# Soft mixture-of-experts logits: factor applied to phi's columns in place of the products, softmaxes on the products in PSUM, division by the sums moved to the combine stage

## The chip, the core and the metric

One Trainium2 chip; the program runs on one core. The metric is the device time of one execution in microseconds (us). The time given for a kernel is the median of its runs; one further execution is recorded by the hardware profiler.

## What is computed

The program takes 1250 nodes of 768 features (`x`) and a list of 40000 edges and puts four layers one after another, each added to x: a graph attention layer, a soft mixture of experts, a graph convolution and a top-2 mixture of experts. The change is inside the second, which is, cut to what matters:

```python
# x: 1250 x 768 rows after layer norm; phi: 768 x 32 experts x 32 slots; EPS = 1e-12
xn = l2norm(x, axis=2)
phin = scale * l2norm(phi, axis=0)
logits = einsum('bld,des->bles', xn, phin)
d_w = softmax(logits, axis=-1)                        # over the 32 slots of an expert
c_w = softmax(logits.reshape(b, l, E * S), axis=-1)   # over all 1024
slots = einsum('bld,bles->besd', xn, d_w)
h = gelu(einsum('besd,edh->besh', slots, w1) + b1, approximate=False)
eo = (einsum('besh,ehd->besd', h, w2) + b2).reshape(b, E * S, d)
out = einsum('bkd,blk->bld', eo, c_w)
```

## The kernel before

The kernel is written engine by engine: in each stage a function opens a scope of buffers and semaphores and gives every engine its own list of instructions, with the waits between engines written by hand. At the end of a scope the semaphores are cleared and all engines meet in a barrier (`Scope.clear`, L93). Nothing is scheduled by a planner; the order on each engine is the order of the text, and a wait holds up everything behind it on its engine. TensorE is PE, VectorE is DVE, ScalarE is ACT in what follows.

The rows are tiled as 10 blocks (`NB`) of 128 nodes, the features as 6 slices (`KD`) of 128, and the 1024 slots (`SE`) are the columns. The soft mixture consists of these stages:

- `norm_rows` (L357) makes layer norm and l2 norm of the rows in `R.H`.
- `soft_logits` (L1045) loads phi in 6 slices into `ph` (the tile `slotsT`, later overwritten with the slots) and makes both softmaxes. Its result is `disp`, 10 blocks of 128x1024, and `comb`, the same shape.
- `soft_slots` (L1192) multiplies `R.H` and `disp` to the slots and at its start has the first hidden weights loaded.
- `soft_experts` (L1222) runs the 32 experts in 8 groups of 4, with their weights loaded group by group, the outer ones into the room of `disp`. Its output `eo` is in `R.H`.
- `soft_combine` (L1328) turns each block of `comb` and multiplies it with `eo`; DVE adds the products to `R.X` (L1359).

In `soft_logits` the sum of squares of each column of phi comes first: ACT squares each slice (L1120), PE adds over the partitions with a matrix of ones into the bank pair `psO[1]` (L1151). DVE clips it (L1076), ACT takes the root (L1137), and DVE makes the factor r of each column: a reciprocal (L1081), a correction step (L1082 to L1085) and the scale (L1087). r is the same on all partitions.

The loop over blocks has two slots, s = 0 and 1, each with its own rows, turned rows and PSUM banks. The order on each engine for a block b is:

- PE: transposes of the next block's rows (`turn`, L1157), then 12 matmuls of 128x512 (24 records in the profile) of turned rows and phi into `psO[s]` (`multiply`, L1165). Before them it waits for the turned rows (`s_turned`) and for `s_scaled` >= b + 1, which DVE raises with L1095 of block b - 2, that is when it has taken over the products of the block that used this bank pair. The first two counts come from a bare increment at the start and from the clip.
- ACT: the copy of rows two blocks ahead (L1124), the copy of the turned rows (L1127), then the two exponentials of block b: of all 1024 logits less the row's maximum into `comb`, with their sum in `rs` (L1131), and of the logits less each expert's maximum, in `disp` (L1132). It waits for DVE's subtraction (`s_sub`).
- DVE: the products times r into `sq` (L1095), each expert's maximum (L1099), the row's maximum (L1100) and its negation (L1101), the subtraction (L1102); a wait for both exponentials (`s_exp`); the sum over each expert (L1105), its reciprocal (L1106), the division of `disp` (L1107); the reciprocal of the row's sum (L1108) and the division of `comb` (L1109). `Chain` puts a semaphore wait behind an instruction whose result the next one on the same engine needs; `chain.loop(i, n)` counts these per turn of the loop.

Of the kernel before, what the change touches and what calls it, by code (L numbers as in the profile page):

```python
# [16 lines left out]
ALU = mybir.AluOpType  # L17
# [1024 lines left out]
HC = HID // 2  # L1042


def soft_logits(nc, R, name, phi, scale, disp, comb, ph):  # L1045

    with Scope(nc, name) as c:
# [2 lines left out]
        ones, sc = c.sb("ones", [P, P]), c.sb("scale", [P, 1])  # L1052
        rows = [c.sb(f"rows{s}", [P, D]) for s in range(2)]
        rowsT = [c.sb(f"rowsT{s}", [P, KD, P]) for s in range(2)]
        gm, rm, gs, rs = c.sb("gm", [P, 2, EXPERTS, 1]), c.sb("rm", [P, 2]), c.sb("gs", [P, 2, EXPERTS, 1]), c.sb("rs", [P, 2])
        psT = [c.ps(f"psT{s}", [P, 2, BANK]) for s in range(2)]
        psO = [c.ps(f"psO{s}", [P, 2, BANK]) for s in range(2)]
        s_w = [c.sem(f"weights{k}") for k in range(KD)]
        s_sc, s_v, s_sq, s_n, s_clip, s_root = (c.sem(x) for x in ("scale", "v", "sq", "n", "clip", "root"))
        s_rows, s_turn, s_turned, s_mm, s_scaled, s_exp, s_sub = (c.sem(x) for x in ("rows", "turn", "turned", "mm", "scaled", "exp", "sub"))  # L1060
        block = c.enter_context(nc.Block())

        @block.sync
# [5 lines left out]
        @block.vector  # L1069
        def _(dve):  # L1070
            chain = Chain(dve, s_v)
            chain(nc.vector.memset(ones[:], 1.0))
            dve.sem_inc(s_scaled, 1)
            dve.wait_ge(s_n, KD)
            n2, r = f[:, 0, :], f[:, 1, :]
            chain(nc.vector.tensor_scalar(n2.rearrange("p (a b) -> p a b", a=2), psO[1][:], 1e-24, None, ALU.max))  # L1076
            dve.sem_inc(s_scaled, 1)
            dve.sem_inc(s_clip, 1)
            dve.wait_ge(s_root, 1)

            chain(nc.vector.reciprocal(r, sq[:, 0, :]))  # L1081
            chain(nc.vector.tensor_tensor(sq[:, 1, :], r, r, ALU.mult))  # L1082
            chain(nc.vector.tensor_tensor(sq[:, 1, :], sq[:, 1, :], n2, ALU.mult))
            chain(nc.vector.tensor_scalar(sq[:, 1, :], sq[:, 1, :], -0.5, 1.5, ALU.mult, ALU.add))
            chain(nc.vector.tensor_tensor(r, r, sq[:, 1, :], ALU.mult))  # L1085
            dve.wait_ge(s_sc, 16)
            chain(nc.vector.tensor_scalar(r, r, sc[:], None, ALU.mult))  # L1087

            with dve.Fori(0, NB // 2) as i:
                chain.loop(i, 14)  # L1090
                for s in range(2):

                    b = i * 2 + s
                    dve.wait_ge(s_mm, b + 3)
                    nc.vector.tensor_tensor(sq[:, s, :].rearrange("p (a e) -> p a e", a=2), psO[s][:], r.rearrange("p (a e) -> p a e", a=2), ALU.mult).then_inc(s_scaled, 1)  # L1095
                    dve.wait_ge(s_scaled, b + 3)
                    lg = sq[:, s, :].rearrange("p (e s) -> p e s", e=EXPERTS)
                    dsp = blk(disp, b).rearrange("p (e s) -> p e s", e=EXPERTS)
                    chain(nc.vector.tensor_reduce(gm[:, s], lg, AX.X, ALU.max))  # L1099
                    chain(nc.vector.tensor_reduce(rm[:, s:s + 1], gm[:, s].squeeze(2), AX.X, ALU.max))  # L1100
                    chain(nc.vector.tensor_scalar(rm[:, s:s + 1], rm[:, s:s + 1], -1.0, None, ALU.mult))  # L1101
                    nc.vector.tensor_tensor(dsp, lg, gm[:, s].broadcast_to([P, EXPERTS, SLOTS]), ALU.subtract).then_inc(s_sub, 1)  # L1102
                    dve.wait_ge(s_exp, b * 2 + 2)
                    dve.nop(nofuse=True)
                    chain(nc.vector.tensor_reduce(gs[:, s], dsp, AX.X, ALU.add))  # L1105
                    chain(nc.vector.reciprocal(gs[:, s], gs[:, s]))  # L1106
                    nc.vector.tensor_tensor(dsp, dsp, gs[:, s].broadcast_to([P, EXPERTS, SLOTS]), ALU.mult)  # L1107
                    chain(nc.vector.reciprocal(rs[:, s:s + 1], rs[:, s:s + 1]))  # L1108
                    chain(nc.vector.tensor_scalar(blk(comb, b), blk(comb, b), rs[:, s:s + 1], None, ALU.mult))  # L1109
            chain.end(NB // 2)  # L1110

        @block.scalar
        def _(act):
            act.sem_inc(s_turn, 2)
            act.sem_inc(s_mm, 2)
            for k in range(KD):
                act.wait_ge(s_w[k], 16)
                if k >= 2:
                    act.wait_ge(s_n, k - 1)
                nc.scalar.activation(sq[:, k % 2, :], ph[:, k, :], ACT.Square).then_inc(s_sq, 1)  # L1120

            def turn(b, s):
                act.wait_ge(s_turn, b + 1)
                nc.scalar.copy(rows[s][:], blk(R.H, b)).then_inc(s_rows, 1)  # L1124
                act.wait_ge(s_turn, b + 3)
                act.wait_ge(s_mm, b + 1)
                nc.scalar.copy(rowsT[s][:].rearrange("p (a k) q -> p a (k q)", a=2), psT[s][:, :, 0:HALF]).then_inc(s_turned, 1)  # L1127

            def exponentials(b, s):
                act.wait_ge(s_sub, b + 1)  # L1130
                nc.scalar.activation(blk(comb, b), sq[:, s, :], ACT.Exp, bias=rm[:, s:s + 1], accum_out=rs[:, s:s + 1]).then_inc(s_exp, 1)  # L1131
                nc.scalar.activation(blk(disp, b), blk(disp, b), ACT.Exp).then_inc(s_exp, 1)  # L1132

            turn(0, 0)
            turn(1, 1)
            act.wait_ge(s_clip, 1)
            nc.scalar.activation(sq[:, 0, :], f[:, 0, :], ACT.Sqrt).then_inc(s_root, 1)  # L1137
            with act.Fori(0, NB // 2 - 1) as i:
                for s in range(2):
                    turn(i * 2 + s + 2, s)  # L1140
                    exponentials(i * 2 + s, s)
            for s in range(2):
                exponentials(NB - 2 + s, s)

        @block.tensor
        def _(pe):
            pe.wait_ge(s_v, 1)
            for k in range(KD):
                pe.wait_ge(s_sq, k + 1)
                for a in range(2):  # L1150
                    last = nc.tensor.matmul(psO[1][:, a, :], ones[:], sq[:, k % 2, a * BANK:(a + 1) * BANK], start=(k == 0), stop=(k == KD - 1))  # L1151
                last.then_inc(s_n, 1)

            def turn(b, s):
                pe.wait_ge(s_rows, b + 1)
                for k in range(KD):
                    last = nc.tensor.transpose(psT[s][:, k // 3, (k % 3) * P:(k % 3 + 1) * P], rows[s][:, k * P:(k + 1) * P], R.ident[:])  # L1157
                last.then_inc(s_turn, 1)

            def multiply(b, s):  # L1160
                pe.wait_ge(s_turned, b + 1)
                pe.wait_ge(s_scaled, b + 1)
                for a in range(2):
                    for k in range(KD):
                        last = nc.tensor.matmul(psO[s][:, a, :], rowsT[s][:, k, :], ph[:, k, a * BANK:(a + 1) * BANK], start=(k == 0), stop=(k == KD - 1))  # L1165
                last.then_inc(s_mm, 1)

            turn(0, 0)
            with pe.Fori(0, NB // 2 - 1) as i:
                turn(i * 2 + 1, 1)  # L1170
                multiply(i * 2, 0)
                turn(i * 2 + 2, 0)
                multiply(i * 2 + 1, 1)
            turn(NB - 1, 1)
            multiply(NB - 2, 0)
            multiply(NB - 1, 1)

# [147 lines left out]
                last.then_inc(s_e, 1)  # L1325


def soft_combine(nc, R, name, comb, eo):  # L1328

    with Scope(nc, name) as c:  # L1330
        rows = [c.sb(f"rows{s}", [P, SE]) for s in range(2)]
# [19 lines left out]
        @block.vector  # L1351
        def _(dve):
            dve.sem_inc(s_add, 2)
            with dve.Fori(0, NB // 2) as i:
                for s in range(2):
                    b = i * 2 + s
                    dve.wait_ge(s_mm, b + 3)
                    x = blk(R.X, b).rearrange("p (a d) -> p a d", a=2)
                    nc.vector.tensor_tensor(x, x, psO[s][:, :, 0:HALF], ALU.add).then_inc(s_add, 1)  # L1359

        @block.tensor
        def _(pe):
# [4 lines left out]
                last.then_inc(s_turn, 1)  # L1367

            def multiply(b, s):
                pe.wait_ge(s_add, b + 1)  # L1370
                pe.wait_ge(s_turned, b + 1)
                for a in range(2):
                    for k in range(KS):
# [760 lines left out]
def program(nc, A, out):  # L2134
    with ExitStack() as ctx:
# [51 lines left out]
        norm_rows(nc, R, "ln1", l2=True)  # L2187
        with ExitStack() as soft:
            comb = soft.enter_context(nc.sbuf_tensor("comb", [P, NB, SE], F32))
            slotsT = soft.enter_context(nc.sbuf_tensor("slotsT", [P, KD, SE], F32))  # L2190
            disp = soft.enter_context(nc.sbuf_tensor("disp", [P, NB, SE], F32))
            soft_logits(nc, R, "m1", A["L0_ffn_phi"], A["L0_ffn_scale"], disp, comb, slotsT)
            eo = R.H
            with Scope(nc, "hw") as c:
                hidden_weights = HiddenWeights(c, A["L0_ffn_w1"])
                soft_slots(nc, R, "m2", disp, slotsT, hidden_weights)
                soft_experts(nc, R, "m3", hidden_weights, A["L0_ffn_b1"], A["L0_ffn_w2"], A["L0_ffn_b2"], slotsT, eo, disp[:])
            soft_combine(nc, R, "m4", comb, eo)
        with ExitStack() as gcn:
            R.high = gcn.enter_context(nc.sbuf_tensor("high", [P, NB, D], FR))  # L2200
            R.low = nc.alloc_sbuf_tensor_at("low", [P, NB, D], FR, offset=h_at)
# [39 lines left out]
```

## Time and profile before

| what | value |
|---|---|
| median of 3 runs | 4810.34 us (4807.37 to 4814.28) |
| the profiled execution, time | 4806.03 us |
| its span, first to last instruction | 4803.5 us |
| mean granted clock of PE | 0.922 of full speed |
| PE busy, share of the span | 3900.7 us, 81% |
| DVE busy | 2679.1 us, 56% |
| ACT busy | 1793.9 us, 37% |
| POOL busy | 1492.7 us, 31% |

The page gives shares over the whole span; the stages have very different limits, so it is the stage that is to be read. In the rows below, a line of a timeline reads: start in us from the span's start, duration in us, engine, line of the kernel, operation, output<-inputs, count, and in brackets the engine's idle time before it with what ended that. A line of the windows reads: stretch, its length, then busy us (and count) of PE, PE's weight loads, DVE, ACT and POOL, the granted clock of PE as a share of full speed, the share of DMA and GB/s. A line of the groups reads: line, engine, operation, output<-inputs with shapes, count, busy us, mean ns of one, idle time before them with its releasers. Ends of PE's matmuls are modelled.

### The profile page before, as it was taken

The page shows a single profiled execution, that of the slowest core. Times are in us where ns is not written, and L with a number is a line of the kernel's source. Part 1 is how long each engine was busy: PE and PEld are TensorE (multiplying, and loading weights), DVE is VectorE, ACT ScalarE, POOL GpSimd, SP SyncE. Part 2 cuts the span into 40 slices and gives each one's busy share as a digit, 9 for nine tenths or more (in the row PEclk, how much of TensorE's full clock was granted, in tenths as well). Part 3 has the DMA queues.
Part 4 walks back from the last instruction along what each step waited for, and adds up shares of the span by engine and source line. Part 5 has one row for each costly group of instructions (what it writes and reads, how often), then busy time and mean ns, then how long its engine had stood idle before and what let it go on. Part 6 is the DMA issues. An engine that isn't in the chain of part 4 may idle for free. (4 is left out here: it accounts for less than half of the span.)

```text
span 4803.5 us, 77604 instructions
## 1 busy us (share of the span) xinstructions
PE 3900.7 (81%) x19093; PEld 2693.1 (56%) x19094; DVE 2679.1 (56%) x8404; ACT 1793.9 (37%) x4836; POOL 1492.7 (31%) x1513
## 2 busy tenths in 40 slices
PE   6989996599975888885877809859588996599999
PEld 4566664344433466664555504325587776488887
DVE  4489999677785367767777786000897213011010
ACT  0067775377761022221666623001896101111111
POOL 0155553477750155553777700000000000211110
PEclk9999998699997999997999959979899996799999
DMA  3278884388862378775888810180000001634342
GB/s 108 78 253 270 271 268 154 109 273 272 270 205 82 86 257 260 255 257 178 277 262 262 266 42 8 40 309 0 0 0 16 8 24 66 258 116 165 104 156 91
DMA packets 204806, 765.45 MB, mean 159 GB/s; under 512 B 36862, under 2 KB 60270, under 8 KB 204734
## 3 DMA queue, kind: packets, MB, share of 16 engines
q0 software_dynamic: 119328, 566.15, 36.8%
q1 hardware_dynamic: 82334, 194.49, 11.6%
q10 hardware_dynamic: 3072, 3.94, 0.3%
q8 instruction: 35, 0.57, 0.1%
q14 instruction: 37, 0.30, 0.0%
HBM read 838.08 MB, written 26.53 MB: 180 GB/s over the span
## 5 line engine op out<-in xcount | busy, mean ns | idle before, releaser
L689 PE MATMUL l_psZ<-X,ident 128*128 128x396 f32 (+3 forms) x2656 | 811.5, 428 | 0.4 <-issue 0.3
L887 POOL DMA_INDIRECT a_g<-fs,pair_src x664 | 716.5, 1079 | 304.2 <-issue 162.0
L625 POOL DMA_INDIRECT X<-fs,near_src x664 | 627.9, 946 | 481.8 <-DVE l_zr L657 167.1
L963 PE MATMUL a_psO<-a_g,a_sel 128*128 128x396 f32 (+1 forms) x1992 | 726.2, 509 | 43.7 <-DVE a_g L911 31.2
L689 PEld LDWEIGHTS l_psZ<-X,ident 128*128 128x128 f32 x2656 | 498.5, 191 | 189.4 <-issue 5.9
L942 ACT ACTIVATE a_g<-a_g,L 128x99 f32<-128x99 f32 (+1 forms) x1494 | 529.1, 428 | 182.4 <-DMA a_g<-fs,pair_src 169.2
L686 PE MATMUL l_psZ<-fd,l_spread 128*128 x1328 | 449.4, 418 | 150.4 <-DVE l_zr L659 69.2
L963 PEld LDWEIGHTS a_psO<-a_g,a_sel 128*128 128x128 f32 x1992 | 376.2, 195 | 314.8 <-issue 120.4
L919 DVE TENSOR_TENSOR acc<-acc,a_psO 128x386 f32 (+2 forms) x664 | 342.9, 558 | 238.3 <-PE a_psO L963 180.3
L686 PEld LDWEIGHTS l_psZ<-fd,l_spread 128*128 128x128 f32 x1328 | 235.1, 190 | 230.4 <-issue 210.3
L2117 PEld LDWEIGHTS r_psH<-r_rowsT,r_w 128*128 128x128 f32 x2916 | 331.2, 193 | 17.4 <-DMA r_w<-in_L_ffn_w 10.5
L2117 PE MATMUL r_psH<-r_rowsT,r_w 128*128 128x128 f32 x2916 | 331.5, 276 | 10.1 <-DMA r_w<-in_L_ffn_w 10.1
L652 DVE SCALAR_TENSOR_TENSOR l_zr<-l_psZ,l_attn 128x99 f32<-128x99 f32 x1660 | 327.2, 255 | 4.2 <-issue 3.3
L608 ACT ACTIVATE l_zr<-l_zr 128x99 f32<-128x99 f32 x996 | 271.6, 274 | 136.9 <-DVE l_zr L657 98.1
L646 DVE TENSOR_TENSOR l_psZ<-l_psZ,X 128x124 f32<-128x124 f32 (+1 forms) x664 | 216.3, 326 | 184.1 <-PE l_psZ L689 142.1
L2127 PE MATMUL r_psY<-r_w,r_hT 128*128 128x384 f32 x972 | 318.0, 486 | 0.0
L659 DVE SCALAR_TENSOR_TENSOR l_zr<-l_psZ,l_attn 128x772 f32<-128x772 f32 x332 | 315.9, 952 | 0.0
L1531 PE MATMUL ec_psC<-ec_sel,ec_pick 128*128 128x128 bf16 x3920 | 229.4, 220 | 83.3 <-DVE ec_pick L1496 42.6
L602 ACT ACTIVATE l_spread<-l_away,l_one 128x512 fp32r<-128x512 f32 x166 | 119.9, 722 | 426.8 <-PE l_psZ L689 355.0
L1531 PEld LDWEIGHTS ec_psC<-ec_sel,ec_pick 128*128 128x128 bf16 x3920 | 221.3, 98 | 91.9 <-issue 49.9
L2127 PEld LDWEIGHTS r_psY<-r_w,r_hT 128*128 128x128 f32 x972 | 182.6, 190 | 121.6
L2060 ACT ACTIVATE r_hT<-r_psH,r_b1t 128x128 f32<-128x128 f32 x243 | 87.8, 367 | 380.7 <-PE r_psH L2117 379.6
(393 smaller groups left out, 5437.0 us busy)
## 6 DMA issues: line engine op xcount, KB each, us to landing
r_w<-in_L_ffn_w SPq DMA_DIRECT2D x54, 3456.0 KB
l_dsts<-near_rows SPq DMA_DIRECT2D x166, 128.0 KB
hw_w<-in_L_ffn_w SPq DMA_DIRECT2D x8, 2304.0 KB
disp<-in_L_ffn_w SPq DMA_DIRECT2D x8, 2304.0 KB
X<-fs,near_src POOLq DMA_INDIRECT x664
a_g<-fs,pair_src POOLq DMA_INDIRECT x664
H<-in_L_ffn_b SPq DMA_DIRECT2D x27, 384.0 KB
X<-in_x SPq DMA_DIRECT2D x2, 3456.0 KB
```

Of the source, the lines that this page charges most:

```text
L625: nc.gpsimd.indirect_dma_start(out=g[:, n % RING, :], out_offset=None, in_=fs, in_offset=bass.IndirectOffsetOnAxis(ap=R.near_src[:, n:n + ...
L652: nc.vector.scalar_tensor_tensor(out=zr[:, k, lo:hi], in0=psZ[k][:, lo // half, lo % half:lo % half + he], scalar=0.0, in1=at[:, lo:hi], o ...
L659: last = nc.vector.scalar_tensor_tensor(out=zr[:, k, :].rearrange("p (a e) -> p a e", a=2), in0=psZ[k][:, :, 0:half], scalar=0.0, in1=at[: ...
L686: nc.tensor.matmul(psZ[k][:, a, 0:half], spread[:, j // 4, k, :], R.fd[:, ds(b, 1), lo:hi].squeeze(1), start=True, stop=True)
L689: last = nc.tensor.matmul(psZ[k][:, a, 0:hi - lo], R.ident[:], g[:, j, lo:hi], start=False, stop=True, skip_group_check=True)
L887: nc.gpsimd.indirect_dma_start(out=g[:, n % RING, 0:width], out_offset=None, in_=table, in_offset=bass.IndirectOffsetOnAxis(ap=R.pair_src[ ...
L919: nc.vector.tensor_tensor(acc, acc, psO[j][:, a, 0:hi - lo], ALU.add).then_inc(s_add, 1)
L942: last = nc.scalar.activation(rows, rows, ACT.Copy, scale=R.L[:, h, ds(v * 2 + 1, 1)])
L963: last = nc.tensor.matmul(psO[j][:, a, 0:hi - lo], sel[:, j, k, :].bitcast(F32), g[:, j * 2 + k, lo:hi], start=(k == 0), stop=(k == 1))
L1531: last = nc.tensor.matmul(psC[s][:, b * P:(b + 1) * P], pick[:, s, k, b * P:(b + 1) * P], sel[:, s, k, :], start=(k == 0), stop=(k == WIDE ...
L2117: last = nc.tensor.matmul(psH[m % 4][:, 0:P], w1t[s][:, k, m * P:(m + 1) * P], rowsT[s][:, k, :], start=(k == 0), stop=(k == KD - 1))
L2127: last = nc.tensor.matmul(psY[:, a, 0:HALF], hT[s][:, m, :], w2t[s][:, m, a * HALF:(a + 1) * HALF], start=(m == 0), stop=(m == KH - 1))
```

## The change

- r is no longer applied to the products. DVE multiplies the six slices of phi by r in place, each product raising the new semaphore `s_ph`, and PE waits for all six before the first products.
- L1095 goes, and with it `s_scaled`. The maxima and the subtraction read the products in `psO[s]`, and ACT's exponential into `comb` reads them there too.
- PE's wait before block b is now for `s_exp` >= 2b + 1: ACT raises it by 4 at the start and by one with each exponential, so that it stands for the exponential into `comb` of block b - 2.
- The sum of that exponential goes to a new tile `sums` (128x10, one column a block), which lives until the combine stage. L1108 and L1109 go.
- In `soft_combine` DVE takes the reciprocal of `sums` at the start, and the addition becomes a multiply-add with the block's column. PE's wait for `s_add` counts one more, for that reciprocal.

```diff
 def soft_logits(...)
...
+            for k in range(KD):
+                nc.vector.tensor_tensor(ph[:, k, :], ph[:, k, :], r, ALU.mult).then_inc(s_ph, 1)
 
             with dve.Fori(0, NB // 2) as i:
-                chain.loop(i, 14)
+                chain.loop(i, 10)
                 for s in range(2):
                     b = i * 2 + s
                     dve.wait_ge(s_mm, b + 3)
-                    nc.vector.tensor_tensor(sq[:, s, :].rearrange("p (a e) -> p a e", a=2), psO[s][:], r.rearrange("p (a e) -> p a e", a=2), ALU.mult).then_inc(s_scaled, 1)
-                    dve.wait_ge(s_scaled, b + 3)
-                    lg = sq[:, s, :].rearrange("p (e s) -> p e s", e=EXPERTS)
+                    lg = psO[s][:].rearrange("p a (e s) -> p (a e) s", s=SLOTS)
...
-                    dve.wait_ge(s_exp, b * 2 + 2)
+                    dve.wait_ge(s_exp, b * 2 + 6)
...
                     nc.vector.tensor_tensor(dsp, dsp, gs[:, s].broadcast_to([P, EXPERTS, SLOTS]), ALU.mult)
-                    chain(nc.vector.reciprocal(rs[:, s:s + 1], rs[:, s:s + 1]))
-                    chain(nc.vector.tensor_scalar(blk(comb, b), blk(comb, b), rs[:, s:s + 1], None, ALU.mult))
...
         @block.scalar
+            act.sem_inc(s_exp, 4)
...
-                nc.scalar.activation(blk(comb, b), sq[:, s, :], ACT.Exp, bias=rm[:, s:s + 1], accum_out=rs[:, s:s + 1]).then_inc(s_exp, 1)
+                nc.scalar.activation(blk(comb, b).rearrange("p (a e) -> p a e", a=2), psO[s][:], ACT.Exp, bias=rm[:, s:s + 1], accum_out=sums[:, ds(b, 1)]).then_inc(s_exp, 1)
...
             def multiply(b, s):
                 pe.wait_ge(s_turned, b + 1)
-                pe.wait_ge(s_scaled, b + 1)
+                pe.wait_ge(s_ph, KD)
+                pe.wait_ge(s_exp, b * 2 + 1)
...
 def soft_combine(...)
...
             dve.sem_inc(s_add, 2)
+            nc.vector.reciprocal(sums[:], sums[:]).then_inc(s_add, 1)
+            dve.wait_ge(s_add, 3)
...
-                    nc.vector.tensor_tensor(x, x, psO[s][:, :, 0:HALF], ALU.add).then_inc(s_add, 1)
+                    nc.vector.scalar_tensor_tensor(out=x, in0=psO[s][:, :, 0:HALF], scalar=sums[:, ds(b, 1)], in1=x, op0=ALU.mult, op1=ALU.add).then_inc(s_add, 1)
...
-                pe.wait_ge(s_add, b + 1)
+                pe.wait_ge(s_add, b + 2)
```

## Rows read from the trace of the kernel before

**Rows 1.** Windows by stage: norm's end and logits; combine.
```profile
2868.00:3018.00 150.00, 123.54 (x324) 57.10 (x324) 95.40 (x122) 49.95 (x61) 0.00 (x0) 0.91 0.06 21
...
3239.00:3361.00 122.00, 116.07 (x400) 71.51 (x400) 9.55 (x11) 19.69 (x21) 0.00 (x0) 0.96 0.00 0
```

**Rows 2.** Timeline of DVE, head of the logits stage.
```profile
2893.32 1.23 DVE L1076 TENSOR_SCALAR m_f<-m_psO 128x1024 f32<-128x1024 f32 x1 [18.25 <-PE m_psO L1151]
2898.26 6.55 DVE L1081 RECIPROCAL m_f<-m_sq 128x1024 f32<-128x1024 f32 x1 [3.71 <-ACT m_sq L1137]
...
2909.35 0.76 DVE L1087 TENSOR_SCALAR m_f<-m_f,m_scale 128x1024 f32<-128x1024 f32 x1
2910.33 1.22 DVE L1095 TENSOR_TENSOR m_sq<-m_psO,m_f 128x1024 f32<-128x1024 f32 x1 [0.23 <-DVE m_f L1087]
```

**Rows 3.** Timeline of PE, from phi's squares to the last products.
```profile
2879.96 13.33 PE L1151 MATMUL m_psO<-m_sq,m_ones 128*128 128x512 f32 x24 [107.49 <-ACT m_sq L1120]
...
2895.56 0.87 PE L1157 MATMUL m_psT<-ident,m_rows 128*128 128x128 f32 x6 [1.62 <-ACT m_rows L1124]
2896.27 10.47 PE L1165 MATMUL m_psO<-slotsT,m_rowsT 128*128 128x512 f32 x24
...
2907.23 10.46 PE L1165 MATMUL m_psO<-slotsT,m_rowsT 128*128 128x512 f32 x24
...
2929.73 0.88 PE L1157 MATMUL m_psT<-ident,m_rows 128*128 128x128 f32 x6 [0.88 <-ACT m_rows L1124]
...
2985.23 20.77 PE L1165 MATMUL m_psO<-slotsT,m_rowsT 128*128 128x512 f32 x48
```

**Rows 4.** Timeline of DVE in the loop, the first instruction of two successive blocks.
```profile
2931.90 1.22 DVE L1095 TENSOR_TENSOR m_sq<-m_psO,m_f 128x1024 f32<-128x1024 f32 x1 [0.45 <-DVE comb L1109]
...
2942.52 1.23 DVE L1095 TENSOR_TENSOR m_sq<-m_psO,m_f 128x1024 f32<-128x1024 f32 x1
```

**Rows 5.** Timeline of DVE, the last block of the logits stage.
```profile
3007.06 1.23 DVE L1095 TENSOR_TENSOR m_sq<-m_psO,m_f 128x1024 f32<-128x1024 f32 x1
3008.32 1.22 DVE L1099 TENSOR_REDUCE m_gm<-m_sq 128x32 f32<-128x1024 f32 x1
...
3010.11 1.23 DVE L1102 TENSOR_TENSOR disp<-m_sq,m_gm 128x1024 f32 x1 [0.17 <-DVE m_rm L1101]
...
3015.30 1.23 DVE L1107 TENSOR_TENSOR disp<-disp,m_gs 128x1024 f32 x1
3016.44 0.15 DVE L1108 RECIPROCAL m_rs<-m_rs 128x1 f32<-128x1 f32 x1
3016.72 0.75 DVE L1109 TENSOR_SCALAR comb<-comb,m_rs  x1
```

**Rows 6.** Windows of 2 us around two restarts of PE, at 2879.96 and 3018.44.
```profile
2884.00:2886.00 2.00, 2.00 (x4) 0.85 (x3) 0.00 (x0) 0.87 (x1) 0.00 (x0) 0.61 0.20 66
...
3008.00:3010.00 2.00, 0.00 (x0) 0.00 (x0) 1.84 (x4) 0.00 (x0) 0.00 (x0) 0.61 0.00 0
...
3020.00:3022.00 2.00, 2.00 (x4) 0.69 (x3) 0.00 (x0) 0.00 (x0) 0.00 (x0) 0.50 0.84 327
3022.00:3024.00 2.00, 2.00 (x6) 1.00 (x5) 0.00 (x0) 0.00 (x0) 0.00 (x0) 0.97 1.02 422
```

**Rows 7.** Timeline of PE, start of the slots stage, up to 3030 us.
```profile
3018.44 11.93 PE L1212 MATMUL m_ps<-disp,H 128*128 128x512 f32 x23 [12.44 <-PEq L96]
```

**Rows 8.** Groups by form: the logits stage's Exp, the combine stage's copies and addition, a multiply-add.
```profile
L1131 ACT ACTIVATE comb<-m_sq,m_rm 128x1024 f32 x8 | 9.2, 1148 | 38.3 <-DVE disp L1102 38.3
...
L1346 ACT COPY m_rows<-comb 128x1024 f32 x10 | 10.5, 1047 | 11.3 <-ACTq L1340 11.3
L1349 ACT COPY m_rowsT<-m_psT 128x1024 f32<-128x1024 f32 x10 | 10.1, 1012 | 80.0 <-PE m_psT L1366 80.0
L1359 DVE TENSOR_TENSOR X<-X,m_psO 128x768 f32 x10 | 9.5, 954 | 112.3 <-PE m_psO L1374 112.3
...
L141 DVE SCALAR_TENSOR_TENSOR H<-H,f_rstd,f_bias 128x768 f32<-128x768 f32 x20 | 18.8, 1014 | 0.1
```

More of the change, by code:

```diff
@@ L1042, with soft_logits @@
 HC = HID // 2
-def soft_logits(nc, R, name, phi, scale, disp, comb, ph):
+def soft_logits(nc, R, name, phi, scale, disp, comb, ph, sums):
     with Scope(nc, name) as c:
@@ L1054, in soft_logits @@
         rowsT = [c.sb(f"rowsT{s}", [P, KD, P]) for s in range(2)]
-        gm, rm, gs, rs = c.sb("gm", [P, 2, EXPERTS, 1]), c.sb("rm", [P, 2]), c.sb("gs", [P, 2, EXPERTS, 1]), c.sb("rs", [P, 2])
+        gm, rm, gs = c.sb("gm", [P, 2, EXPERTS, 1]), c.sb("rm", [P, 2]), c.sb("gs", [P, 2, EXPERTS, 1])
+        s_ph = c.sem("ph")
         psT = [c.ps(f"psT{s}", [P, 2, BANK]) for s in range(2)]
@@ L1059, in soft_logits @@
         s_sc, s_v, s_sq, s_n, s_clip, s_root = (c.sem(x) for x in ("scale", "v", "sq", "n", "clip", "root"))
-        s_rows, s_turn, s_turned, s_mm, s_scaled, s_exp, s_sub = (c.sem(x) for x in ("rows", "turn", "turned", "mm", "scaled", "exp", "sub"))
+        s_rows, s_turn, s_turned, s_mm, s_exp, s_sub = (c.sem(x) for x in ("rows", "turn", "turned", "mm", "exp", "sub"))
         block = c.enter_context(nc.Block())
@@ L1072, in _ @@
             chain(nc.vector.memset(ones[:], 1.0))
-            dve.sem_inc(s_scaled, 1)
             dve.wait_ge(s_n, KD)
@@ L1076, in _ @@
             chain(nc.vector.tensor_scalar(n2.rearrange("p (a b) -> p a b", a=2), psO[1][:], 1e-24, None, ALU.max))
-            dve.sem_inc(s_scaled, 1)
             dve.sem_inc(s_clip, 1)
@@ L1325, in _, with soft_combine @@
                 last.then_inc(s_e, 1)
-def soft_combine(nc, R, name, comb, eo):
+def soft_combine(nc, R, name, comb, eo, sums):
     with Scope(nc, name) as c:
@@ L2189, in program @@
             comb = soft.enter_context(nc.sbuf_tensor("comb", [P, NB, SE], F32))
+            sums = soft.enter_context(nc.sbuf_tensor("sums", [P, NB], F32))
             slotsT = soft.enter_context(nc.sbuf_tensor("slotsT", [P, KD, SE], F32))
             disp = soft.enter_context(nc.sbuf_tensor("disp", [P, NB, SE], F32))
-            soft_logits(nc, R, "m1", A["L0_ffn_phi"], A["L0_ffn_scale"], disp, comb, slotsT)
+            soft_logits(nc, R, "m1", A["L0_ffn_phi"], A["L0_ffn_scale"], disp, comb, slotsT, sums[:])
             eo = R.H
@@ L2197, in program @@
                 soft_experts(nc, R, "m3", hidden_weights, A["L0_ffn_b1"], A["L0_ffn_w2"], A["L0_ffn_b2"], slotsT, eo, disp[:])
-            soft_combine(nc, R, "m4", comb, eo)
+            soft_combine(nc, R, "m4", comb, eo, sums[:])
         with ExitStack() as gcn:
```

## The prediction

> **What bounds the kernel now.** I read the windows by stage first, because every stage ends in a barrier of all engines: a gain or a loss inside one moves everything behind it by as much. The changed code lies in the stretch of 150 us up to 3018 us, which holds the end of the norm and the logits stage, and in the 122 us of the combine stage; both keep PE busy for most of their time [rows 1]. The slots and experts stages between them are untouched.
>
> Then the timeline of the head of the logits stage, DVE and PE side by side. DVE gets the sums of squares of phi at 2893.32 us. From there ACT and DVE make r, the factor of each column: clip, square root, a reciprocal of 6.55 us, four correction steps, the scale. r is finished at 2909.35 + 0.76 = 2910.11 us [rows 2]. PE does not wait for it: it turns block 1 at 2895.56 and starts the products of block 0 at 2896.27 us, 14 us before r exists [rows 3]. **This head start is what the reader is to see**: the products are made with unscaled phi and multiplied by r afterwards, so r is wanted only by DVE.
>
> Then the loop. PE needs 10.47 us for the 24 matmul records of a block and 10.96 us from one block's start to the next (2907.23 less 2896.27). From block 0's start to block 8's it takes 2985.23 - 2896.27 = 88.96 us, 1.3 us more than 8 x 10.96 = 87.68: it lost that at blocks 2 and 3, where ACT's copy of rows came late, the larger part in one gap of 0.88 us [rows 3]. DVE needs nearly as long: 10.62 us from one block's first instruction to the next (2931.90 to 2942.52) [rows 4]. So the loop is PE's, with DVE hardly shorter. PE's last matmul ends at 2985.23 + 20.77 = 3006.00 [rows 3]; DVE turns to that block only at 3007.06, since it was still on block 8, and needs till 3016.72 + 0.75 = 3017.47 [rows 5]. Those 11.5 us are the tail that no PE work covers.
>
> **The change part by part.**
> *Scaling phi in place.* Six DVE products of 128x1024 from SBUF to SBUF join the chain behind r. The like operation lasts 1.23 us (L1107), and one with no wait before it starts 1.14 us after the former (3015.30 to 3016.44) [rows 5]. Five steps of 1.14 and one whole: 6.9 us. With the first where L1095 stands now, 2910.33 [rows 2], phi is ready at 2917.3 us. PE now waits for all six before block 0 and starts some 0.2 us after the release, as L1095 does after r: 2917.5. That is **+21.2 us** against 2896.27. Queued behind that wait on PE are all products and the turning of block 2 onwards; DVE's first reduction and ACT's second copy of that turning wait for them in turn. Nothing else is to be done in that time, so it is paid in full.
> The Trainium skill (VectorE: DVE Perf Modes, "The DRAIN you can't avoid") says that the next operation starts only once the pipe is empty, with or without a semaphore between. By that rule the six would take 6 x 1.26, about 7.6 us, an estimate with the step of chained operations (3007.06 to 3008.32), and the loss would be 0.7 us larger. The rows have the next one start 0.09 us before the end of the former, so the sum goes by them.
>
> *The clock.* PE has nothing to do from 2896.4 to 2917.5 us. In the pause after 3006 the granted clock fell to 0.61 between 3008 and 3010; at the restart it was 0.50 (1.2 GHz) until 3022 and 0.97 after, so low for some 3.6 us of work [rows 6]. The 23 matmul records from that restart took 11.93 us [rows 7]; at 10.47 us for 24 they take 10.0 [rows 3]. So **+1.9 us**. Bounds: 0 if the clock should stay up; 2.9 from the start at 2879.96, where it was low for some 5.7 us [rows 3, 6]. The pause before the slots stage shrinks from 12.4 us to about 9.6, but the clock fell within 4 us of the former, so that start stays as slow as it is.
>
> *The loop.* DVE loses L1095 (1.23 us), the reciprocal L1108 (0.15) and L1109 (0.75) [rows 5]: with their gaps a block falls to some 8.3 us, and DVE then waits for PE's products at each. PE's 10.96 us stand, as the number of matmuls does, and its two delays go, because ACT's exponentials no longer come late: **-1.3 us**. The rest of DVE's gain, some 2.3 us a block, becomes idle time and is worth nothing. The cover is PE's 10.96 us; without it each us of DVE's would count.
> Each product bank is now held until ACT has read it. DVE's two reductions and the negation take 1.79 us (3008.32 to 3010.11), the subtraction 1.23 [rows 5], ACT's Exp 1.15 [rows 8]: free some 4.4 us after the products, and PE comes back to it after 10.96. The new wait costs nothing, with 6 us to spare.
>
> *Reading PSUM.* The reduction, the subtraction and the Exp now read PSUM. Nearest rows: L1095, a PSUM reader, 1.22 and 1.23 us [rows 2, 5], against 1.23 for the SBUF reader L1107 [rows 5]; ACT's copies, 1.012 from PSUM (L1349) against 1.047 from SBUF (L1346) [rows 8]. I take 0; the bounds are -0.04 us and +0.1 us, on the last block alone.
> The Trainium skill (VectorE: DVE Perf Modes, "The TRN2 errata") gives VectorE a fixed cost of 120 cycles for a source in PSUM and 58 for SBUF, 65 ns more for each of two operations. That would speak against the change and make the tail 0.13 us longer. The trace disagrees, with 1.22 and 1.23 us.
>
> *The tail.* DVE begins 0.03 us after PE's end, as at L1076 (2879.96 + 13.33 = 2893.29, then 2893.32) [rows 2, 3], in place of 1.06: **-1.0 us**. L1095 goes with its step (3007.06 to 3008.32: 1.26) and so does all behind L1107's end (3017.47 - 3016.53: 0.94): **-2.2 us** [rows 5].
>
> *Combine stage.* A reciprocal of 128x10 comes at its start, between 0.15 us (128x1) [rows 5] and 6.55 (128x1024) [rows 2] and far nearer the first; the wait that counts it is that of the second product block, some 19 us into the stage, so even the upper bound costs nothing. L1359 becomes a multiply-add: 0.954 us now, 1.014 for L141, a multiply-add of that size [rows 8]. Nine of ten lie beside PE, whose matmuls fill the stage; the last gives +0.06, **+0.1** rounded up. No DMA is added, and none is moved past a queue.
>
> *Sum:* 21.2 + 1.9 - 1.3 - 1.0 - 2.2 + 0.1 = **+18.7 us**. The profiled execution took 4806.0 us (span 4803.5): it should come to 4824.7 (4822.2). The median of the runs shown is 4.3 us above that execution, so 4810.3 + 18.7 = **4829 us**, 0.39% slower. A measurement of this kernel can tell about 0.2%, 9.6 us, from no change.
>
> **The rivals.**
> *A, not slower: DVE really sets the loop.* DVE's 10.6 us and PE's 10.96 are near enough that the banks handed back by DVE could be what paces PE. Then the loop would drop to DVE's new 8.3 us or so: nine steps of 2.6 less are 23 us, and the sum is about -5, **4806 us**. It decides from the point where PE's own work takes less than 10.96 - 18.7 / 9 = 8.9 us a block. Against it: blocks 8 and 9 run as one row of 48 matmul records in 20.77 us, 10.4 each without turning, the same pace as ever, and no row of PE shows a wait for DVE [rows 3]. 4 in 100.
> *B, the low clock lasts through all of block 0:* 10.4 us more where I have 1.9, so +8.5, **4837.5 us**. For it: after the pause before 2879.96 the low clock lasted 5.7 us, not 3.6. Against: at both restarts it was over within 6 us [rows 3, 6]. 5 in 100.
> *C, the rest of the program hides it:* the three runs shown lie 6.9 us apart, so another set could be some 5 us lower; with no clock cost (-1.9) and PE's start 2 us earlier the difference could fall below 9.6 us, about **4819 us**. 7 in 100, of which 2 would be faster.
> The forecast has 84 in 100. Slower by over 0.2%: the forecast, B, and 1 of C: 90. Within 0.2%: A and the middle of C: 8. Faster: 2.
>
> **The range.** The forecast's own bounds (clock 0 to 2.9 us, scaling 6.9 to 7.6, PSUM, multiply-add) and the spread of the runs, 3 us under and 4 over the median, give 4823 to 4835. Reaching up to B and part of the way down to C: 4821 to 4838.
>
> **What would show it right or wrong.** In the changed kernel's timeline: six products writing slotsT between some 2910.3 and 2917.3 us; PE idle from 2896.4 until then and the first products after it; granted clock 0.5 at their start; then 10.96 us a block without a gap; waits of DVE for PE's products, of some 2.5 us a block, where it had none; the last DVE instruction 8.3 us after the last product, at about 3036; the slots stage beginning at about 3037.1 in place of 3018.4, and each later stage as much later. I am wrong if PE's step changes (A), if the first block takes over 15 us (B), or if the stages behind are shifted by other than the logits stage's loss.

## The result and the profile after

The changed kernel took 4826.09 us, the median of 13 runs (4819.92 to 4832.41), the kernel before 4812.69 us in 13 runs beside it: ratio 1.0029, 95% interval 1.0020 to 1.0037. That is slower by 13.4 us, between 9.6 and 17.8. Forecast were 4829 us and a loss of 18.7 us: the time lies 3 us above the measured one, the loss just above the interval. The execution profiled after the change took 4819.92 us, the shortest of its 13, with a span of 4818.0, against 4806.03 and 4803.5 before.

The timeline of DVE in the changed kernel, head of the logits stage, answers [rows 2]:

```profile
2908.85 0.75 DVE L1086 TENSOR_SCALAR m_f<-m_f,m_scale 128x1024 f32<-128x1024 f32 x1
2909.64 6.90 DVE L1088 TENSOR_TENSOR slotsT<-slotsT,m_f 128x1024 f32<-128x1024 f32 x6
2929.78 1.22 DVE L1098 TENSOR_REDUCE m_gm<-m_psO 128x32 f32<-128x1024 f32 x1 [13.24 <-PE m_psO L1164]
```

The new line is L1088: six products, 6.90 us in all. Behind it DVE waits 13 us for PE, which had been ahead of it before. The timeline of PE over the same stage answers [rows 3]:

```profile
2880.45 12.33 PE L1149 MATMUL m_psO<-m_sq,m_ones 128*128 128x512 f32 x24 [107.45 <-ACT m_sq L1118]
...
2895.06 0.87 PE L1155 MATMUL m_psT<-ident,m_rows 128*128 128x128 f32 x6 [1.62 <-ACT m_rows L1122]
2916.81 12.93 PE L1164 MATMUL m_psO<-slotsT,m_rowsT 128*128 128x512 f32 x24 [20.88 <-DVE slotsT L1088]
...
2930.23 10.47 PE L1164 MATMUL m_psO<-slotsT,m_rowsT 128*128 128x512 f32 x24
...
2941.19 10.46 PE L1164 MATMUL m_psO<-slotsT,m_rowsT 128*128 128x512 f32 x24
...
3006.93 20.77 PE L1164 MATMUL m_psO<-slotsT,m_rowsT 128*128 128x512 f32 x48
```

The third row is the result in one line: PE idle for 20.88 us, released by DVE's scaling, and a first block of 12.93 us in place of 10.47. From the second block on the step is 10.96 us to the last ((3006.93 - 2930.23) / 7), with no gap. In the windows of 2 us at that start the granted clock is half until past 2920, as in [rows 6]:

```profile
2918.00:2920.00 2.00, 2.00 (x4) 0.82 (x3) 0.00 (x0) 0.00 (x0) 0.00 (x0) 0.50 0.00 0
2920.00:2922.00 2.00, 2.00 (x4) 0.81 (x3) 0.00 (x0) 0.00 (x0) 0.00 (x0) 0.60 0.00 0
2922.00:2924.00 2.00, 2.00 (x7) 0.80 (x6) 0.00 (x0) 0.00 (x0) 0.00 (x0) 1.00 0.00 0
```

DVE's last block, for [rows 5], and its combine stage, for [rows 8], from the timeline of DVE:

```profile
3027.74 1.23 DVE L1098 TENSOR_REDUCE m_gm<-m_psO 128x32 f32<-128x1024 f32 x1 [2.14 <-PE m_psO L1164]
...
3029.54 1.22 DVE L1101 TENSOR_TENSOR disp<-m_psO,m_gm 128x1024 f32 x1 [0.17 <-DVE m_rm L1100]
...
3034.69 1.22 DVE L1106 TENSOR_TENSOR disp<-disp,m_gs 128x1024 f32 x1
...
3254.45 0.22 DVE L1353 RECIPROCAL sums<-sums 128x10 f32<-128x10 f32 x1 [1.18 <-PEq L96]
3272.82 1.02 DVE L1360 SCALAR_TENSOR_TENSOR X<-m_psO,sums,X 128x768 f32 x1 [18.15 <-PE m_psO L1375]
```

DVE begins 0.04 us after PE's end (3006.93 + 20.77 = 3027.70) and is done 8.2 us later. Reading PSUM costs nothing: 1.22 to 1.23 us, as from SBUF.

**Stage by stage.** The stages are cut at rows of the timelines: logits from DVE's memset (L1072, in the changed kernel L1073) to the first matmul of the slots stage; slots from there to the first load of outer weights (L1249); experts to ACT's first copy of `comb` (L1346); combine to the next norm's first DVE row. The second pair is one more profile of each kernel, on another chip; its logits stages are given in full.

| us | before | after | difference | second pair, difference |
|---|---|---|---|---|
| up to the stage | 2874.9 | 2875.4 | +0.5 | -9.0 |
| logits | 143.5 | 161.3 | **+17.7** | 142.1, 160.6: **+18.5** |
| slots | 106.3 | 106.7 | +0.4 | 107.3, 106.6: -0.7 |
| experts | 115.2 | 111.3 | **-3.9** | 115.6, 111.5: **-4.1** |
| combine | 121.0 | 119.7 | -1.3 | 119.6, 119.7: +0.1 |
| the rest | 1442.5 | 1443.6 | +1.1 | 1443.3, 1444.0: +0.7 |

The logits stage lost what was forecast. The surprise is the experts stage, in which no instruction was changed and which became some 4 us shorter. The windows of that stage, before and then after, say that its DMA moves more a second (last column, GB/s) at the same share of time:

```profile
3124.78:3239.97 115.19, 60.20 (x664) 26.98 (x664) 11.73 (x25) 9.66 (x41) 0.00 (x0) 0.78 0.93 322
```

```profile
3143.38:3254.71 111.33, 60.53 (x664) 27.24 (x664) 11.95 (x26) 9.76 (x42) 0.00 (x0) 0.80 0.93 333
```

So the runs had two questions: whether the logits stage loses by the lost head start and the clock alone, and what shortens the experts stage.

### The profile page after: what moved, and what is told of

The parts are those of the page before. It is cut to its first block and busy times, and to the rows that moved or that the text cites. A ratio compares the mean times of both kernels' runs of the same rounds, so it can differ in the third digit from the quotient of the medians.

```text
span 4818.0 us, 77555 instructions
## 1 busy us (share of the span) xinstructions
PE 3898.3 (81%) x19093; PEld 2692.3 (56%) x19094; DVE 2666.4 (55%) x8381; ACT 1791.5 (37%) x4836; POOL 1491.6 (31%) x1513
## 3 DMA queue, kind: packets, MB, share of 16 engines
q10 hardware_dynamic: 3072, 3.94, 0.3%
## 5 line engine op out<-in xcount | busy, mean ns | idle before, releaser
L686 PE MATMUL l_psZ<-fd,l_spread 128*128 x1328 | 452.7, 421 | 143.5 <-DVE l_zr L659 66.4
L963 PEld LDWEIGHTS a_psO<-a_g,a_sel 128*128 128x128 f32 x1992 | 372.7, 193 | 316.8 <-issue 115.3
L961 PE MATMUL a_psO<-a_high,a_sel 128*128 128x386 f32 x332 | 135.3, 408 | 116.7 <-DVE a_low L906 98.0
```

The lines of the kernel that those rows point to most:

```text
L686: nc.tensor.matmul(psZ[k][:, a, 0:half], spread[:, j // 4, k, :], R.fd[:, ds(b, 1), lo:hi].squeeze(1), start=True, stop=True)
L963: last = nc.tensor.matmul(psO[j][:, a, 0:hi - lo], sel[:, j, k, :].bitcast(F32), g[:, j * 2 + k, lo:hi], start=(k == 0), stop=(k == 1))
```

## The experiments

They ran on several chips, on which the kernel before takes 4575 to 4845 us; nearly all of that difference lies ahead of the logits stage, which starts at 2647 us on one of them and at 2917 on another. So whole times are compared by their ratio to the kernel before on the same chip, and stages by their own length. A stage's length is from one profile each: from PE's first product to its end the logits stage of the kernel before, with or without an unused tile (experiments 7 and 8), is 122.2 us in all six profiles of it, while the part ahead of that product varies from 19.9 to 21.7.

**1. No scaling of phi, no wait for it.** This leaves out the six products: the logits are those of unscaled phi.

```diff
             dve.sem_inc(s_clip, 1)
+            dve.sem_inc(s_ph, 1)
...
-            for k in range(KD):
-                nc.vector.tensor_tensor(ph[:, k, :], ph[:, k, :], r, ALU.mult).then_inc(s_ph, 1)
...
-                pe.wait_ge(s_ph, KD)
+                pe.wait_ge(s_ph, 1)
```

> The six products that scale phi are left out, and PE's first products wait only for the clip, so the logits are those of unscaled phi; all else is the changed kernel. Theory: the loss is PE's late start (21.0 us, from 41.4 to 20.4 us after the stage's first instruction) and its half clock at the start (2.5 us), nothing else. Then block 0 starts 20.4 us into the stage and takes 10.5 us, the step stays 10.96, and the logits stage, 161.3 us in the changed kernel and 143.5 in the one before, takes 137.8 us; the whole about 4826 - 23.5 = 4802.5. Rival (DVE sets the step): the step falls to 8.4 us and the stage to some 115 us. Rival (part of the loss lies in the softmaxes' reading of PSUM): the stage stays over 139.1, that is 143.5 less the 4.4 us which the shorter DVE work should give.

Measured: logits stage 138.4 us, ratio 0.9985 (0.9976 to 0.9994). PE's timeline:

```profile
2666.85 0.87 PE L1154 MATMUL m_psT<-ident,m_rows 128*128 128x128 f32 x6 [1.62 <-ACT m_rows L1121]
2667.56 10.46 PE L1163 MATMUL m_psO<-slotsT,m_rowsT 128*128 128x512 f32 x24
...
2678.52 10.46 PE L1163 MATMUL m_psO<-slotsT,m_rowsT 128*128 128x512 f32 x24
```

PE starts 21.0 us into the stage (20.4 expected; the squares ahead of it vary) and steps at 10.96 though DVE is now free of all scaling. That fells the rival that DVE sets the step: with DVE's work cut to 8.2 us a block, the step did not move by 0.01 us. The stage is 0.6 us longer than expected and 0.7 below the bound of the PSUM rival. The loss lies in the wait for phi and the slow start behind it, all of it.

**2. A wait for each slice.**

```diff
-                pe.wait_ge(s_ph, KD)
...
                     for k in range(KD):
+                        if a == 0:
+                            pe.wait_ge(s_ph, k + 1)
                         last = nc.tensor.matmul(...)
```

> PE waits for each slice of phi by itself, before the first matmul that reads it, in place of all six before the first. Theory: PE starts 5 x 1.14 = 5.7 us earlier, DVE's 1.14 us a slice stays ahead of PE's 1.7 us at half clock, and the stage is 161.3 - 5.7 = 155.6 us. Rival: waits among the matmuls stretch the loop of all ten blocks, a step above 10.96, and eat the gain; 0.1 us a wait would be 6 us in ten blocks. Whole: 4820 against 4826.

Measured: stage 155.4 us, ratio 1.0020 (1.0011 to 1.0029). From PE's timeline:

```profile
2686.50 12.53 PE L1165 MATMUL m_psO<-slotsT,m_rowsT 128*128 128x512 f32 x24 [15.08 <-DVE slotsT L1088]
...
2699.53 10.46 PE L1165 MATMUL m_psO<-slotsT,m_rowsT 128*128 128x512 f32 x24
...
2710.48 10.04 PE L1165 MATMUL m_psO<-slotsT,m_rowsT 128*128 128x512 f32 x23
```

The idle time falls from 20.88 to 15.08 us, by the 5.8 of five products, and the 60 waits in the loop cost nothing: the step stays 10.96. About a third of the stage's loss could be had back by the placing of one wait. In the whole time the interval reaches to the changed kernel's 1.0029, so it is the stage that shows this.

**3. PE kept at work during the wait.**

```diff
             turn(0, 0)
+            turn(1, 1)
+            pe.wait_ge(s_clip, 1)
+            for _ in range(23):
+                nc.tensor.matmul(psO[0][:, 0, :], ones[:], f[:, 0, 0:BANK], start=True, stop=True)
             with pe.Fori(0, NB // 2 - 1) as i:
-                turn(i * 2 + 1, 1)
                 multiply(i * 2, 0)
                 turn(i * 2 + 2, 0)
                 multiply(i * 2 + 1, 1)
+                turn(i * 2 + 3, 1)
-            turn(NB - 1, 1)
```

> While PE waits for phi it runs 23 idle matmuls of 128x512 (ones times the clipped squares, into the first product bank, overwritten afterwards). Theory: they take 23 x 0.857 = 19.7 us of the 21 us pause, the clock stays at 1.00, block 0 takes 10.5 us in place of 12.9, and the stage is 161.3 - 2.5 = 158.8 us. Rival: the slow first block isn't the clock's doing (reads of phi beside DVE's writes, for example): it stays at 12.9. Rival: the idle matmuls slow DVE's scaling beside them, and PE starts later than 41.4 us into the stage.

Measured: stage 159.6 us, ratio 1.0029 (1.0019 to 1.0040). PE's timeline, then DVE's:

```profile
2667.99 19.91 PE L1171 MATMUL m_psO<-m_f,m_ones 128*128 128x512 f32 x46
2689.01 10.56 PE L1164 MATMUL m_psO<-slotsT,m_rowsT 128*128 128x512 f32 x24 [1.11 <-DVE slotsT L1088]
```

```profile
2681.86 6.90 DVE L1088 TENSOR_TENSOR slotsT<-slotsT,m_f 128x1024 f32<-128x1024 f32 x6
```

With the pause filled, block 0 takes 10.56 us, 2.4 less than in the changed kernel, and the windows give a granted clock of 1.00 from 2664 to 2700 us, pause and block 0 included: the slow first block is the clock's. DVE's six products still take 6.90 us beside PE's work. The stage is 0.8 us over the expectation because PE starts 42.1 us into it, where 41.4 was taken. 2.4 us are too little for the whole time to tell.

**4. Head start for the first two blocks.** phi is loaded into the last six blocks of `disp`, blocks 0 and 1 multiply it raw, their products are scaled in PSUM, and the scaled phi goes to `slotsT`.

```diff
+        raw = disp[:, NB - KD:NB, :]
...
+                nc.vector.tensor_tensor(ph[:, k, :], raw[:, k, :], r, ALU.mult).then_inc(s_ph, 1)
+            for s in range(2):
+                dve.wait_ge(s_mm, s + 3)
+                nc.vector.tensor_tensor(psO[s][:], psO[s][:], r.rearrange("p (a e) -> p a e", a=2), ALU.mult).then_inc(s_scaled, 1)
...
+            turn(0, 0)
+            turn(1, 1)
+            pe.wait_ge(s_clip, 1)
+            multiply(0, 0, raw)
+            turn(2, 0)
+            multiply(1, 1, raw)
+            pe.wait_ge(s_ph, KD)
```

> phi is loaded into the room of the last six blocks of the dispatch weights; blocks 0 and 1 multiply it unscaled and have their products multiplied by r in PSUM, the scaled phi is written to slotsT beside that, and blocks 2 to 9 use it as in the changed kernel. Theory: PE has its head start again (start 20.4 us into the stage), the clock stays up, DVE is one block behind at first and catches up by 2.5 us a block, the tail is the short one: the stage is near 143.5 - 4.4 = 139 us, up to 2 more for the bank of block 1, the whole some 4 us below the kernel before, 4808. Rival: DVE's lag of 11 us at block 0 holds the banks and PE waits for them at blocks 2 and 3, by up to 8 us: stage 147, no gain over before.

Measured: stage 147.9 us, ratio 1.0005 (0.9996 to 1.0013). The rival came true in its size, and PE's timeline names what held it:

```profile
2679.27 10.46 PE L1177 MATMUL m_psO<-disp,m_rowsT 128*128 128x512 f32 x24
2696.23 1.54 PE L1169 MATMUL m_psT<-ident,m_rows 128*128 128x128 f32 x6 [6.49 <-ACT m_rows L1136]
2697.56 12.48 PE L1177 MATMUL m_psO<-slotsT,m_rowsT 128*128 128x512 f32 x24
```

PE waits 6.49 us for ACT's copy of the rows of block 3. On ACT that copy stands behind the exponentials of block 0, and they wait for DVE, which scales phi first:

```profile
2682.18 6.90 DVE L1089 TENSOR_TENSOR slotsT<-disp,m_f 128x1024 f32<-128x1024 f32 x6
2689.00 1.22 DVE L1108 TENSOR_TENSOR m_psO<-m_psO,m_f 128x1024 f32<-128x1024 f32 x1
```

The pause also cost the clock: block 2 takes 12.48 us. The head start was won and half of its gain given back: from PE's first product the stage is 126.7 us, where without any scaling (experiment 1) it is 117.4; of these 9.3 us the wait is 6.5 and the clock 2.0. The whole time is that of the kernel before, though the logits stage is 4.0 us longer than the longest of that kernel (143.9); this kernel has `sums` too, with the tiles behind it moved (experiment 7). It was the order on ACT, not the bank named in the expectation, that the profile shows as the last wait.

**5. The division alone.** The kernel before, with only `sums` and the combine stage of the change (the multiply-add and PE's count as in the change, not shown again).

```diff
+            sums = soft.enter_context(nc.sbuf_tensor("sums", [P, NB], F32))
...
-                    chain(nc.vector.reciprocal(rs[:, s:s + 1], rs[:, s:s + 1]))
-                    chain(nc.vector.tensor_scalar(blk(comb, b), blk(comb, b), rs[:, s:s + 1], None, ALU.mult))
...
-                nc.scalar.activation(blk(comb, b), sq[:, s, :], ACT.Exp, bias=rm[:, s:s + 1], accum_out=rs[:, s:s + 1]).then_inc(s_exp, 1)
+                nc.scalar.activation(blk(comb, b), sq[:, s, :], ACT.Exp, bias=rm[:, s:s + 1], accum_out=sums[:, ds(b, 1)]).then_inc(s_exp, 1)
...
             dve.sem_inc(s_add, 2)
+            nc.vector.reciprocal(sums[:], sums[:]).then_inc(s_add, 1)
+            dve.wait_ge(s_add, 3)
```

> The kernel before with one part of the change alone: the sums of the combine weights go to the new tile, L1108 and L1109 go, and the combine stage divides; phi is not scaled and r stays on the products. Theory: PE keeps its head start; DVE's block is 1.2 us shorter, so that it isn't late for the last block (-1.0), the tail is 0.94 us shorter, PE's two delays (1.3) shrink in part: the stage is 143.5 - 2 to 3.2, that is 140.3 to 141.5 us; the combine stage is 0.06 us longer. Whole: 4810 against 4812.7, hardly to be told. Rival: DVE was not the cause of the delays at blocks 2 and 3; then only 1.9 us. In this kernel the tile sums lies where the changed kernel has it: if its experts stage is 111.3 within 0.5 as well, that speaks for the place of the tiles.

Measured: ratio **0.9986** (0.9977 to 0.9995), 4832.7 us against 4840.8: faster than the kernel before, where the whole change is slower. Its logits stage is 140.0 us, the experts stage 111.7. DVE at the last block:

```profile
3036.32 1.23 DVE L1107 TENSOR_TENSOR disp<-disp,m_gs 128x1024 f32 x1
3038.39 1.23 DVE L1095 TENSOR_TENSOR m_sq<-m_psO,m_f 128x1024 f32<-128x1024 f32 x1 [0.84 <-PE m_psO L1163]
...
3046.64 1.23 DVE L1107 TENSOR_TENSOR disp<-disp,m_gs 128x1024 f32 x1
```

DVE now waits for PE at the last block (0.84 us), where it had been late, and the stage ends with L1107. Counted from PE's first product, to leave out the squares ahead of it, the stage is 118.9 us against 122.2 in both profiles of the kernel before: -3.2, the most that was expected. The delay of 1.1 us at block 3 is gone, the 0.2 at block 2 is not. The whole time is 8.1 us shorter. The profiles of that chip give 3.2 of it to this and 3.9 to the experts stage (111.7 against 115.6); slots and combine differ by -1.2 and +1.7, single profiles each. But the ratio doesn't show that moving the division pays: an unused tile alone gives the same 0.9986 (experiment 7). What shows it is the logits stage, -3.2 us. With that said it is the version to keep, at 0.9986 where the whole change is at 1.0029.

**6. Second profiles.**

> The kernel before, for a second profile. The experts stage (from the first load of outer weights to ACT's first copy in the combine stage) took 115.2 us before and 111.3 after the change, though nothing in it was changed; the slots stage 106.3 and 106.7, the combine stage 121.0 and 119.7. Theory: run-to-run scatter of a stage bound by DMA; this run gives an experts stage anywhere from 110 to 116 us. Rival: the change shortens it through the place of the tiles in SBUF; then this run gives 115.2 within 0.5. The logits stage should be 143.5 within 0.3.

> The changed kernel, for a second profile. Scatter: experts stage from 110 to 116 us. Rival (place of the tiles): 111.3 within 0.5. Logits stage 161.3 within 0.3, with block 0 taking between 12.3 and 13.4 us, as the moment at which the clock comes back need not be the same.

Measured: the stages of the table above. The experts stage repeated within 0.5 us in each kernel (115.2 and 115.6; 111.3 and 111.5), so scatter of 110 to 116 is out. The logits stage of before came at 142.1 in place of 143.5, because phi's squares were done 1.5 us earlier; from PE's first product on both are 122.2.

**7. The place of the tiles.** `sums` takes 40 bytes a partition between `comb` and `slotsT`, and all tiles behind it move by 64. `disp`, where the outer weights of the experts land, started at byte 144576 (192 over a multiple of 256) and starts at 144640 (a multiple of 256) after; the hidden weights move alike. Four kernels, all on one chip, differ from the kernel before or the changed one by an unused tile there and nothing else; its width, 16 below for 64 bytes, is 48 for 192 bytes and 8 for 32:

```diff
+            soft.enter_context(nc.sbuf_tensor("room", [P, 16], F32))
             slotsT = soft.enter_context(nc.sbuf_tensor("slotsT", [P, KD, SE], F32))
```

> The kernel before with an unused tile of 64 bytes a partition between comb and slotsT, and nothing else: slotsT, disp and the hidden weights lie 64 bytes further, as in the changed kernel (disp at 144640, a multiple of 256, in place of 144576, which is 192 over one). Theory of place: the experts stage takes 110 to 112 us in place of 115.2 and 115.6, the whole some 4 us less, ratio 0.9991. Rival (something in the instructions of the change): 115.2 to 115.6 and ratio 1. The logits stage stays at 142 to 143.6.

> The changed kernel with an unused tile of 192 bytes behind sums, so that slotsT, disp and the hidden weights stand as they did before, 192 bytes over a multiple of 256. Theory of place: the experts stage takes 115 to 116 us again, the logits stage 160.6 to 161.3 as ever, and the whole is 18 us above the kernel before, ratio 1.0037, where the changed kernel had 1.0029. Rival: 111.3 and 1.0029.

> The kernel before with an unused tile of 192 bytes: the tiles 128 over a multiple of 256. If a multiple of 128 is enough, the experts stage takes 110 to 112 us; if it takes 256, 115 to 116.

> The kernel before with an unused tile of 32 bytes: disp at 144608, 224 over a multiple of 256 and 32 over one of 64. If place works by steps of 64 bytes, the experts stage is longer than 115.6 us; if only the multiple of 256 (or 128) counts, it is 115 to 116.

| kernel | `disp` over a multiple of 256 | experts stage, us | ratio of whole |
|---|---|---|---|
| before, 64 bytes | 0 | 112.7 | 0.9986 (0.9977 to 0.9996) |
| before, 192 bytes | 128 | 112.7 | single run |
| before, 32 bytes | 224 | 115.3 | single run |
| changed, 192 bytes | 192 | 115.0 | 1.0042 (1.0028 to 1.0056) |

The windows of the experts stage, of the first and of the last of these:

```profile
3160.03:3272.68 112.65, 59.50 (x664) 27.01 (x664) 11.73 (x25) 9.66 (x41) 0.00 (x0) 0.80 0.94 329
```

```profile
3186.44:3301.41 114.97, 59.94 (x664) 26.85 (x664) 11.95 (x26) 9.76 (x42) 0.00 (x0) 0.78 0.93 322
```

An unused tile makes the experts stage of the kernel before shorter, and takes the gain away from the changed kernel. With the second profiles it holds on three chips: 115.0 to 115.6 us at places 192 and 224, 111.3 to 112.7 at places 0 and 128. So place is a cause. How much it is worth is less sure: on this one chip it is 2.3 to 2.6 us (115.0 and 115.3 against 112.7). On the chips of the two pairs before and after differ by 3.9 and 4.1, and no kernel with an unused tile was profiled there, so whether the other 1.5 us or so are the chip's or another effect of the change stays open. The whole time can't settle it: with the unused tile of 64 bytes it is shorter by 0.14% (0.04 to 0.23), which is anything from 1.9 to 11 us. The logits stage of the shifted changed kernel was 162.7, 1.4 us over the expectation: PE started 42.3 us in, and block 0, begun at the low clock, took 13.42 us. The ratio 1.0042 fits 1.0037, but its interval reaches down to 1.0028 and alone would not tell it from the changed kernel's 1.0029.

The Trainium skill (DMA: Bandwidth & Descriptors, "How a descriptor splits into AXI transactions") says that a descriptor is split into transactions of 256 bytes, and that the first one of a descriptor which does not start at a multiple of 256 starts at the boundary below it, so that bytes are fetched and not used. For the rows of 3072 and 4608 bytes here that makes one transaction more, an estimate from that section, whether the start is 128, 192 or 224 over. The section is worded for reading, and the tiles moved here are written to. The runs agree for 192 and 224, but 128 over a multiple of 256 was as fast as 0, which that rule doesn't give.

**8. Only the hidden weights moved.**

```diff
             with Scope(nc, "hw") as c:
+                c.sb("room", [P, 16])
                 hidden_weights = HiddenWeights(c, A["L0_ffn_w1"])
```

> The kernel before with an unused tile of 64 bytes between disp and the hidden weights: only the hidden weights (half of the bytes loaded in the experts stage) move to a multiple of 256; slotsT and disp, where the outer weights land, stay at 192 over one. If the place of the hidden weights is what counts, the experts stage takes 110 to 112.7 us; if that of disp, 115.0 to 115.6; if both share, near 114. Logits stage 142 to 144 in any case.

Inconclusive: the experts stage was 112.6 us, in the first of the bands expected, but the ratio was 0.9999 (0.9990 to 1.0008), and the run fell on a chip where the kernel before takes 4577 us. On another chip of about that time (4575 us) the kernels of experiments 1 to 4, with all tiles moved, have 109.9 to 111.4 us, and on neither was an unmoved kernel profiled. The DMA packets in the traces say a little more (the hidden weights are 6 of the stage's 14 loads of 2304 KB). Hidden weights come in packets of 4608 bytes, outer ones of 3072. In the four profiles with all tiles at 192 or 224 a packet of hidden weights took 205 to 209 ns in the mean, in the nine with all at 0 or 128 it took 194 to 204; here, with the hidden weights moved, 201. For the outer weights it is 136 to 138 against 132 to 139, and here, unmoved, 136. So the hidden weights' packets seem to follow their own place, though over chips that differ; for the outer weights the two bands overlap. Whether the outer weights' place counts stays open.

## Why the prediction was right

- **The head start, right to 0.2 us in its own step.** Six products: 6.9 us forecast, 6.90 measured, at 1.14 us from one to the next, where the rule of the Trainium skill (VectorE: DVE Perf Modes, "The DRAIN you can't avoid") gave 7.6; the same section adds that a next operation that isn't held starts earlier, and these six did. They start 0.04 us behind r, where 0.22 were reckoned, and PE 0.27 after their end. PE's first products came 41.4 us into the stage in place of 21.4: +20.0, not +21.2, and 1.0 of that difference is the squares before them, 12.33 us in place of 13.33, which the change doesn't touch. In the second pair it was +21.0.
- **The clock**, +1.9 forecast, +2.5 measured (2.1 to 3.0 in the further profiles with that pause), inside the bounds 0 and 2.9 but for the longest. Experiment 3 shows that it is the clock.
- **The loop**, -1.3, as measured: 10.96 us a block from block 1 on and no gap. Rival A fell with experiment 1. Rival B did not occur: block 0 took 12.5 to 13.4 us in the four profiles with the pause, not 20.
- **Reading PSUM**, 0: 1.22 us for both DVE operations. ACT's Exp went from 1.15 to 1.11, the -0.04 of the bound.
- **The tail**, -1.0 and -2.2: DVE 0.04 us behind PE and done 8.21 us later, where 8.3 were said. One number beside the sum is a slip: PE's pause before the slots stage was put at about 9.6 us, where 12.4 less the two terms of the tail is 9.2; it was 8.97.
- **The combine stage**: reciprocal 0.22 us, hidden; multiply-add 1.02 us, +0.06.
- **The logits stage's sum** was 18.6 without the combine stage; measured +17.7 and +18.5.
- **What failed** is the last sentence of the part on what would show it: "each later stage as much later". The experts stage got 3.9 us shorter. The step behind it is the one that called the stages between untouched and costed the new tile `sums` at nothing: it moves every tile behind it, and DMA into those tiles depends on where they stand. With it, 18.7 - 3.9 = 14.8, against 13.4 measured. Experiment 7 ties 2.3 to 2.6 us of this to the place of the tiles, the rest is open.

The range held and the direction was right with 0.90 on it, though the interval begins at the very bound of 0.2%. The closeness of the time, 4829 against 4826, is in part luck: the kernel before was measured 2.4 us longer beside the changed one than in the runs shown, which offset part of the experts stage's unforeseen gain. As a difference, 18.7 us is 5.3 too much and lies outside 9.6 to 17.8.

## What to carry to other kernels

A factor applied late, to each block's products, can be cheaper than the same factor applied once to the operand: what counts is whether the engine that sets the pace can start without it. Here the removed work was DVE's, which had little slack (10.62 us a block under PE's 10.96), and the added wait was PE's, which had none; the part of the change that took work off DVE without adding a wait made the logits stage 3.2 us shorter. And a new tile, however small, moves all tiles behind it; note the address of every DMA destination before and after, and compare with an unused tile of the same size before a gain or a loss is put down to the code.

## What was not expected of the hardware

A load stage bound by DMA took 115.0 to 115.6 us with its destination tiles 192 or 224 bytes over a multiple of 256, and 111.3 to 112.7 with them 0 or 128 over, at 320 to 322 against 329 to 333 GB/s, over three chips, with weights in rows of 3072 and 4608 bytes. On one of them alone it is 115.0 and 115.3 against 112.7 us. And the kernel before, unused tiles or none, on chips whose whole time differs by 270 us, has logits stages of 142.1 to 143.9 us, and of 122.2 in each from PE's first product on.
